# Straight-line attention on TensorE, FFN inputs loaded two tiles ahead, and two smaller moves in a cross-attention and FFN kernel

## What is computed

```python
x = x + xattn(layernorm(x), ctx, Wq, Wk, Wv, Wo)      # 16 heads of 128, softmax over 256 keys
x = x + ffn(layernorm(x), w_gate, w_up, w_down)       # inner width 2048

def ffn(x, w_gate, w_up, w_down):
    # _mx_linear rounds both operands to a small block float format, one scale for 32 elements
    inter = silu(_mx_linear(x, w_gate)) * _mx_linear(x, w_up)
    return _mx_linear(inter, w_down)
```

## Time and profile before

| | before |
|---|---|
| median of the runs | 2190.7 us |
| the profiled execution | 2190.88 us |
| its span in the trace | 2189.3 us |
| TensorE (PE) busy | 2085.6 us, 95% |
| VectorE (DVE) busy | 1533.2 us, 70% |
| ScalarE (ACT) busy | 1035.8 us, 47% |
| GpSimd (POOL) busy | 791.9 us, 36% |

### The profile page before, as it was taken

The page is one execution under the profiler, slowest core; times in us unless marked ns, Lnnn a source line. Parts: engine busy times, 40 slices in busy tenths (PEclk is TensorE's granted clock), DMA queues, the critical chain, the costliest instruction groups (busy, mean ns, idle before and its releaser), DMA issues.

```text
span 2189.3 us, 49860 instructions
## 1 busy us (share of the span) xinstructions
PE 2085.6 (95%) x15818; PEld 1535.8 (70%) x15818; DVE 1533.2 (70%) x3455; ACT 1035.8 (47%) x2760; POOL 791.9 (36%) x1093
## 2 busy tenths in 40 slices
PE   6899999999999999999999999999999978999996
PEld 5678777877787877777787877787888853444442
DVE  6777776777777776777676767676665548777774
ACT  7755554555555554545454545455544532333331
POOL 4333333332333333333232323331111006666664
PEclk9999999999999999999999999999999998999998
DMA  6733433232333333333333333232232253544444
GB/s 219 185 79 73 83 69 88 64 78 69 79 73 78 74 76 76 76 76 76 72 76 76 76 76 76 67 74 62 61 63 59 52 152 65 85 82 84 84 84 66
DMA packets 398607, 179.55 MB, mean 82 GB/s; under 512 B 361984, under 2 KB 374784, under 8 KB 398400
## 3 DMA queue, kind: packets, MB, share of 16 engines
q1 hardware_dynamic: 375616, 125.10, 27.7%
q0 software_dynamic: 16608, 45.36, 8.5%
q10 hardware_dynamic: 6176, 6.29, 0.9%
HBM read 61.08 MB, written 27.26 MB: 40 GB/s over the span
## 4 chain that ended last, share of the span: by engine, by line
PE 80%; issue 4%; DVE 4%; DMA 4%; POOL 3%; ACT 3%; SPq 1%; POOLq 0%; DVEq 0%; ACTq 0%
PE b_qk L1019 30%; PE b_v L1019 15%; PE b_o L1074 7%; PE b_c L1019 7%; PE b_s L1019 7%; PE b_w L1074 7%; DMA attn_weights<-x_scratch 2%; POOL attn_weights L514 2%; PE b_pt L1019 1%; DMA probT<-psplit 1%; PE b_x L1019 1%; PE b_w L1162 1%; PE b_x L1026 1%; DVE inner_amax L951 1%; SPq L328 1%
## 5 line engine op out<-in xcount | busy, mean ns | idle before, releaser
L559 ACT ACTIVATE qk<-b_qk 128x512 f16<-128x512 f32 x256 | 152.7, 596 | 663.6 <-PE b_s L1019 663.5
L857 DVE TENSOR_REDUCE nmax<-b_s 128x2 f32<-128x512 f32 x257 | 177.7, 691 | 371.9 <-PE b_s L1019 371.9
L1019 PE MATMUL b_qk<-xT,attn_weights 128*128 (+1 forms) x3072 | 382.8, 275 | 25.6 <-issue 23.8
L1019 PE MATMUL b_v<-attn_weights,kvT 128*128 128x256 f16 x3072 | 377.2, 273 | 8.0 <-POOL attn_weights L390 8.0
L1019 PE MATMUL b_qk<-kvT,attn_weights 128*128 (+1 forms) x3072 | 384.6, 276 | 0.0
L1019 PEld LDWEIGHTS b_qk<-xT,attn_weights 128*128 128x128 f16 x3072 | 301.6, 99 | 66.2 <-issue 26.9
L881 DVE SCALAR_TENSOR_TENSOR psplit<-prob,rrec,psplit 128x256 f16<-128x256 f32 x514 | 287.1, 600 | 80.5 <-ACT psplit L600 80.5
L1019 PEld LDWEIGHTS b_qk<-kvT,attn_weights 128*128 128x128 f16 x3072 | 304.4, 99 | 38.5
L1019 PEld LDWEIGHTS b_v<-attn_weights,kvT 128*128 (+1 forms) x3072 | 300.2, 98 | 43.8 <-issue 9.0
L600 ACT ACTIVATE psplit<-prob,rrec 128x256 f16<-128x256 f32 x514 | 233.0, 500 | 95.9 <-DVE rrec L874 95.6
L590 ACT ACTIVATE prob<-b_s,nmax 128x256 f32<-128x256 f32 x514 | 238.8, 469 | 33.3 <-DVE nmax L857 1.6
(11 more groups left out here) (124 smaller groups left out, 2736.7 us busy)
## 6 DMA issues: line engine op xcount, KB each, us to landing
ffn_w<-wffn SPq DMA_DIRECT2D x48, 256.0 KB, 3.2
acc<-xtok POOLq DMA_DIRECT2D x16, 512.0 KB, 4.0
out<-acc POOLq DMA_DIRECT2D x16, 512.0 KB, 4.3
out<-attn_weights POOLq DMA_DIRECT2D x32, 256.0 KB, 4.1
xrow<-xq POOLq DMA_DIRECT2D x61, 128.0 KB, 3.7
kvrow<-kvt POOLq DMA_DIRECT2D x61, 128.0 KB, 3.3
stage<-wattn SPq DMA_DIRECT2D x12, 512.0 KB, 3.8
ffn_scratch<-ffn_t SPq DMA_DIRECT2D x48, 128.0 KB, 1.8
```

Of the source, the lines that this page charges most:

```text
L559: eng.activation(dst, src, ACT.Copy, scale=scale).then_inc(sm[done], 1)
L857: eng.tensor_reduce(nmax[:, :], bS[:, :].rearrange("p (q f) -> p q f", q=2), AX_X, ALU.max, negate=True).then_inc(sm["max_done"], 1)
L1019: last = eng.matmul(out, l, r, start=(a == 0), stop=(a == len(pairs) - 1))
```

## The change

Four edits.

1. TensorE's quads 4 to 63 are straight code; the loop of L1146 is gone. `FFN_FROM` is 4 and `FFN_TO` 52, so each quad has the same instructions in the same order as before.
2. SyncE's FFN order: the load of tile t+2 stands between the two transposes of tile t, where the load of tile t+1 stood ahead of both. Tile 1 is loaded right at the start, as before.
3. The last element's steps move from v = 1 to 6 to v = 5, 6, 8, 9, 11, 13 and 15 on VectorE, and from v = 1, 3, 5, 7 to v = 7, 10, 12, 14, 16 on GpSimd. Tiles 4 to 9 become straight code on these two engines.
4. `gate_up(0, 0, 0)` stands ahead of `context(i, 0)` of the last head but one, not behind it, together with its own waits.

```diff
+LAST_STEPS = {5: (1, 2), 6: (1, 3), 8: (2, 2), 9: (2, 3), 11: (3, 2), 13: (3, 3), 15: (4, 3)}
@@ SyncE
             def tile(t, at, more=True):
+                transpose_inner(2 * t, 2 * at)
                 if more:
-                    load_x_tile(t + 1, 1 - at)
-                for h in range(2):
-                    transpose_inner(2 * t + h, 2 * at + h)
+                    load_x_tile(t + 2, at)
+                transpose_inner(2 * t + 1, 2 * at + 1)
             load_x_tile(0, 0)
             transpose_p(4 * NQ, 0)
+            load_x_tile(1, 1)
             tile(0, 0)
             tile(1, 1)
...
-            tile(TILES - 2, 0)
+            tile(TILES - 2, 0, more=False)
             tile(TILES - 1, 1, more=False)
@@ GpSimd
-                    if last_batch and v == 1:
+                    if last_batch and v == 7:
                         tile_rstd(B - 1)
-                    if last_batch and v == 3:
+                    if last_batch and v == 10:
                         x_round(TILES - 2, 0)
-                    if last_batch and v == 5:
+                    if last_batch and v == 12:
                         x_rescale(TILES - 2)
+                    if last_batch and v == 14:
                         x_round(TILES - 1, 1)
-                    if last_batch and v == 7:
+                    if last_batch and v == 16:
                         x_rescale(TILES - 1)
...
-            tile(2, 0, last_batch=True)
-            tile(3, 1, last_batch=True)
-            with eng.Fori(2, TILES // 2) as m:
+            for t in range(2, 10):
+                tile(t, t % 2, last_batch=True)
+            with eng.Fori(5, TILES // 2) as m:
@@ VectorE (its x1_step calls and its tiles 4 to 9 likewise)
+                    if last_batch and v in LAST_STEPS:
+                        x1_step(B - 1, *LAST_STEPS[v])
@@ TensorE
-            ready(FFN_FROM)
-            quad(FFN_FROM)
-            for q in range(1, QPB + 1):
-                ready(FFN_FROM + q)
-                quad(FFN_FROM + q, ffn=True)
-            with eng.Fori(2, FFN_TO // QPB) as s:
-                for q in range(1, QPB + 1):
-                    ready(QPB * s + q)
-                    quad_at(QPB * s + q, s, q % QPB, ffn=True)
-            for n in range(FFN_TO + 1, NQ):
+            for n in range(FFN_FROM, NQ):
                 if n <= NQ - 4:
                     ready(n)
-                quad(n, prepare=(n < NQ - 4))
+                quad(n, ffn=(FFN_FROM < n <= FFN_TO), prepare=(n < NQ - 4))
...
             eng.wait_ge(sm["v_lo"], i)
-            context(i, 0)
             eng.wait_ge(sm["gate_up_resident"], 16)
             eng.wait_ge(sm["ffn_moved"], FFN_TILES)
             eng.wait_ge(sm["x_lo"], NQ - 4)
             gate_up(0, 0, 0)
+            context(i, 0)
             gate_up(0, 1, 0)
```

More of the change, by code:

```diff
@@ L987, in tile @@
                     round_a(v, h)
[L988 to L1000, removed]
+                    if last_batch and v in LAST_STEPS:
+                        x1_step(B - 1, *LAST_STEPS[v])
             tile(0, 0, begun=2, last_batch=True)
-            for t in range(1, 4):
+            for t in range(1, 10):
                 tile(t, t % 2, last_batch=True)
-            with eng.Fori(2, TILES // 2) as m:
+            with eng.Fori(5, TILES // 2) as m:
                 for a in range(2):
```

## The result

Four runs of the changed kernel gave 2151.35 to 2156.28 us, the median 2155.03; four of the kernel before beside them gave 2190.6 to 2194.46, the median 2191.86. The ratio is 0.9828, with a 95% interval of 0.9811 to 0.9845. So the change gives 1.7%, 36.8 us, where 55.3 were forecast, and the time lies 5 us above the upper end of the range.

A forecast was written before the change was run, and what follows sets the result against it. TensorE was taken as the bound throughout. Gains of 35.6 us in attention, 1.4 up to tile 2 and 18.8 in tiles 2 to 31, less 0.5 in the tail, made 55.3: 2135.5 us predicted, range 2127 to 2150.

The forecast's parts named there:

- the floor: Attention, quads 9 to 52: 44 quads at the straight-code time of 26.86 us each take 1181.8 us, against 1218.17 before.
- Edit 1 has one answer, with bounds of 33 and 36.3: Attention: straight TensorE code gains 35.6 us, between 33 and 36.3, with no other engine's loop taking the stall's place.
- this rival: Attention keeps its stalls (another engine's turn shows, or straight code stalls too); only the FFN gains: 2165 to 2175, chance 0.04.
- any stall of 2 us is left in attention: Attention: a sign set beforehand; if any stall of 2 us remains there, the prediction is wrong.
- The loss: Start of the FFN: the gate product ahead of context makes the last projection 1.4 us later, from 0.5 gained to 2.5 lost.
- the net gain: FFN up to tile 2: 1.4 us gained after the gate product's loss, as the last element's early steps no longer delay tiles.
- the rival with quantising as the bound: FFN stage: quantising, 10.34 us a tile against TensorE's 10.38, becomes the bound at 10.7 to 10.9; 2140 to 2150, chance 0.27.
- Edit 3, second part: Tiles 2 to 31: the last element's moved steps cost TensorE 5.0 us (2 to 10), plus 1.2 for jitter.
- 8 us of waits between tiles 4 and 9: FFN: a sign set beforehand; if TensorE's waits between tiles 4 and 9 exceed 8 us, the prediction is wrong.
- The estimate of 3.7: FFN: the moved steps' excess of 6.4 us, less 0.8 overlap and 1.9 slack, before late clock restart and lengthening.
- such lengthening tells the cases apart: FFN: lengthening of moved steps beside GpSimd separates the forecast from the case against spreading; all at upper bound gives 2140.6.
- The tail: End of the FFN: 0.5 us lost, since a later round of quantising is seen in full.

The follow-up runs named there:

- experiment 1: The changed kernel with VectorE's attention loop (quads 9 to 48) written as straight code too: 2140.63 us, ratio 0.9767.
- experiment 5: The changed kernel with the first gate product put back behind the context product: 2152.49 us.
- experiment 8: The kernel of experiment 1 with the last element's later steps moved on by a half tile or two on VectorE and GpSimd: 2140.84 us.

## Why the prediction was off

**Edit 1: the failed step.** The stalls of TensorE did go, and the floor was right to the digit: 1181.77 us in experiment 1 against 44 x 26.86 = 1181.8. Wrong was "Edit 1 has one answer, with bounds of 33 and 36.3". The prediction named VectorE's four-quad loop, saw that it turns at the same quads, and ruled it out by two numbers: the branch takes 0.06 us, and VectorE is busy 74% of the time. The first is not the price of a turn, since on VectorE the 3.2 us lie behind the branch's record and 1.9 us more at a second place of the body. The second is a mean: it says nothing of whether 2.9 us can be late at one point of a chain whose slack there is some 2.0 (2.9 less the 0.9 that TensorE waits). The rule quoted from the Trainium skill ("Runtime: NRT & Kernel Launch", "Instruction fetch mechanics") is of any engine's taken branch; weighed by it, VectorE's loop would have got a price like TensorE's. I gave this rival a chance of 0.04, and it took 13.8 us. Even so its time of 2165 to 2175 was too high: the changed attention loses some of its stalls, not none, since 2.0 of each 2.9 us are covered. One of the marks that I had set was passed: "any stall of 2 us is left in attention". There are two of 2.2, and the one below.

**Behind quad 53**, 2.9 us. 1.0 is one wait at quad 55. The rest is the last quad, where the transpose beside the resident-weight load lands in 10.7 us, not 9.3, and TensorE waits 5.52, not 4.09:

```profile
1743.30 1.04 PE L1011 MATMUL b_c<-probT,vbuf 128*128 128x256 f16 x4 [5.52 <-DMA probT<-psplit]
```

The prediction took this stretch as unchanged. The wait is 5.5 to 6.4 us in the nine kernels with TensorE's attention straight, and 4.0 to 4.7 in the three with the loop. In all nine a packet of the instruction queue q8 (16 KB, 0.9 to 1.1 us) falls into this transpose, in none of the three. No run moved that packet alone, so the cause stays argued, not shown.

**Edit 4 and the start of the FFN.** The loss was forecast as 1.4 and is 1.8. The gate product waits for tile 0's load, as predicted, and gate_up 2 of tile 1 waits 2.30 us (2.5 forecast). Up to tile 2 the net gain was 3.3 where I had 1.4. Gate_up 2 of tile 1 starts 31.7 us behind the last projection but one, 31.5 before, as forecast. But I had tile 2 another 6.9 to 7.8 us later, a low clock reckoned in, and it came 5.2 us later, because the clock stayed at 1.00 behind the 2.30 us. That is luck: experiment 5 has the same wait with the clock at 0.50 behind it.

**Edit 2** came out as predicted: 10.39 us a tile, no load late. TensorE stays the bound, so the rival with quantising as the bound (0.27) did not come; how large the margin is, for which I had 0.04 us a tile, no run shows.

**Edit 3, second part**: mis-sized, not wrong. 310.47 us against a floor of 301.0 leaves 9.5, where I had 6.2 with bounds up to 10. The mark that I had set myself, 8 us of waits between tiles 4 and 9, was not passed (6.3 us, four times), but these six tiles are 9.1 us over their floor. Some 1.6 of that is the clock, which is at 0.50 from 1838.97 to 1842.38, behind the longest wait and only there; for the last 1.1 I have no cause. The estimate of 3.7 from durations of lone operations left out the blocked 3 us of `x_norm`. I had written that such lengthening tells the cases apart; it did, but for half of the excess only. Without the block (experiment 8) as much was lost elsewhere, and what the steps would cost with neither block nor width no run shows.

**The tail**, 2.3 longer, 0.5 forecast. TensorE's last two products wait 3.31 and 4.14 us where they waited 2.61 and 3.74, and one of 1.03 is new. It is there with edit 2 alone too (39.3 us), where edit 1 alone has 37.8, so it comes with the faster tiles. That the quantising of the last ones no longer keeps up with a TensorE that doesn't wait for loads is how I read it; no run tests it.

The parts add up. Edit 1 alone gives 20.0, edit 2 alone 15.4, undoing edit 3 costs 3.3 and undoing edit 4 gives 2.5: 20.0 + 15.4 + 3.3 - 2.5 = 36.2, against 36.8 for the whole. The 2.5 isn't told apart from noise, so the sum is a check to within some 2 us.

## What to carry to other kernels

When loops of two engines turn at the same point, unrolling one of them buys less than its own stalls (here 20 of 36 us): look at the gap from each engine's branch to its next instruction, not at the branch's length, since a wait "for PE" in the trace of before can cover a stall of the waiting engine itself. Price every engine of the chain that way, and unroll them together, or at least lengthen the body (eight quads for four gave 10.5 us here). Steps that are spread over busy tiles cost about the same there as at the start (here 310 us from tile 2 to 31 either way); spreading pays for the waits that it takes off the path, here 4 us ahead of tile 2.

## What the runs showed of the hardware

- A taken branch on VectorE is recorded as 0.06 us, and the next instruction starts 3.2 us later; a second pause of 1.9 us follows some 3 us further on. An 8 KB packet of queue q14 falls into each pause. With a body twice as long the pauses are 1.9 to 2.3 and 2.2 us. TensorE's branch carries the time in its own record (3.55 us).
- VectorE's operation on 128x32 took 3.32 us beside two of GpSimd's, on 128x512 3.56; with one of them beside it 1.27, and alone 0.55.
- The same transpose doesn't always take the same time: they landed in 3.0 us at best and 4.9 at worst in quads 9 to 52 (view of `probT` in the kernel after), and a long one at a turn is what makes 0.9 us of wait into 2.2:

```profile
DMA to landing us min/median/max: 3.0/3.1/4.9
```

- Long landings go with instruction packets. In quads 9 to 52 of the twelve kernels no transpose without a packet of q8 or q14 between its issue and its landing took over 3.2 us (1474 of them), and each of the 283 that took over 3.4 us had one; 355 others had one and took no longer than 3.4. With TensorE in straight code more transposes take over 3.4 us (13 before, 30 after). No run moved a packet alone, so this is a correlation.
- The same wait of 2.30 us at TensorE was followed by a granted clock of 1.00 in the changed kernel (four matmuls in 1.04 us) and of 0.50 in experiment 5 (1.89 us).
